# Transposing the next tile's attention output inside the last expert of the current tile

## What is computed

```python
# attention with a fixed decay mask per head (16 heads of 64), then a norm over
# each head's 64 channels and all 4096 positions, then the output projection
Q, K, V = (einsum('bld,hde->bhle', ln(x), W) for W in (Wq, Wk, Wv))
out = einsum('bhlm,bhme->bhle', (Q @ K^T) * Dm / sqrt(64), V)
c = head_norm(out) * gn_weight + gn_bias        # statistics over the whole sequence
x = x + c @ Wout
# mixture of experts: 8 routed (top 2, dense weights) and one shared, each 1024 -> 1408 -> 1024
h = ln(x)
combine = top2_softmax(h @ gate_w)
x = x + sum_e combine[e] * (silu(h @ w_gate[e]) * (h @ w_up[e])) @ w_down[e]
x = x + sigmoid(h @ shared_gate_w) * (silu(h @ sw_gate) * (h @ sw_up)) @ sw_down
```

## Time and profile before

| | us |
|---|---|
| median of the runs before | 6355.57 |
| lowest and highest of the two | 5952.12 and 6759.02 |
| the profiled execution | 5947.06 |
| its span, slowest core (core 7) | 5945.5 |
| spans of its eight cores | 5918.0 to 5945.5 |
| mean granted TensorE clock of the cores | 0.901 to 0.905 |

### The profile page before, as it was taken

One profiled execution on the slowest core, in us unless ns is written; L12 is line 12 of the kernel. 1 busy time (PEld: TensorE's weight loads), 2 busy tenths in 40 slices (PEclk: granted clock), 3 DMA queues, 4 the chain that ended last, 5 costly groups with the idle time before them and its releaser, 6 DMA issues.

```text
span 5945.5 us, 65497 instructions; the slowest of 8 cores (5918.0 to 5945.5 us)
## 1 busy us (share of the span) xinstructions
PE 5029.3 (85%) x24644; PEld 2342.1 (39%) x24644; DVE 1437.5 (24%) x3601; ACT 1439.3 (24%) x3555; POOL 190.0 (3%) x333
## 2 busy tenths in 40 slices
PE   3555555589998999899989998999899989998999
PEld 1333333334443444344434443444344434443444
DVE  1455544421112111211121112112211221122111
ACT  1343444221212121212121213121312131213121
POOL 0000000000000000000000000000000000000000
PEclk9666666689998999899989998999899989998999
DMA  8777777523342333343324343424242424242423
GB/s 173 179 180 178 180 184 181 152 93 158 134 153 117 158 134 152 118 160 132 154 116 166 126 156 116 173 117 166 113 166 117 167 114 164 117 169 91 163 117 131
DMA packets 101251, 867.26 MB, mean 146 GB/s; under 512 B 9552, under 2 KB 9552, under 8 KB 65360
## 3 DMA queue, kind: packets, MB, share of 16 engines
q0 software_dynamic: 76048, 787.00, 38.6%
q1 hardware_dynamic: 24896, 76.09, 3.7%
HBM read 837.91 MB, written 103.02 MB: 158 GB/s over the span
## 4 chain that ended last, share of the span: by engine, by line
PE 74%; ACT 3%; DVE 1%; issue 1%; DMA 0%; ACTq 0%; DVEq 0%; SPq 0%
PE psf L1025 25%; PE psf L968 23%; PE psf L972 23%; PE psf L831 2%; ACT silu_sb L984 1%; ACT xln_bf L161 1%; PE psb L750 1%; DVE h_sb L994 1%; ACT ucp_sb L985 1%; DMA x_sb<-x 0%; DVE combT L760 0%; DVE xln2T L764 0%; ACT L151 0%; ACT sqdump L132 0%; ACT sqdump L135 0%
## 5 line engine op out<-in xcount | busy, mean ns | idle before, releaser
L1025 PE MATMUL psf<-wring,h_sb 128*128 128x512 bf16 x6336 | 1464.7, 395 | 153.1 <-DVE h_sb L994 153.1
L968 PE MATMUL psf<-xln2T,wring 128*128 128x512 bf16 x6336 | 1510.2, 381 | 0.3 <-issue 0.2
L972 PE MATMUL psf<-xln2T,wring 128*128 128x512 bf16 x6336 | 1503.5, 380 | 0.0
L984 ACT ACTIVATE silu_sb<-psf 128x512 bf16<-128x512 f32 x792 | 472.9, 597 | 3288.9 <-PE psf L972 3288.9
L1025 PEld LDWEIGHTS psf<-wring,h_sb 128*128 128x128 bf16 x6336 | 636.0, 101 | 981.7 <-issue 301.7
L994 DVE TENSOR_TENSOR h_sb<-silu_sb,ucp_sb 128x512 bf16<-128x512 bf16 x792 | 336.9, 425 | 2429.4 <-ACT ucp_sb L985 2429.4
L972 PEld LDWEIGHTS psf<-xln2T,wring 128*128 128x128 bf16 x6336 | 622.2, 98 | 755.1 <-issue 13.4
L968 PEld LDWEIGHTS psf<-xln2T,wring 128*128 128x128 bf16 x6336 | 622.0, 98 | 754.0 <-issue 13.5
L1041 DVE SCALAR_TENSOR_TENSOR x_sb<-psf,c_sb,x_sb 128x512 f32<-128x512 f32 x576 | 432.6, 751 | 1120.1 <-PE psf L1025 1120.1
L985 ACT CAST ucp_sb<-psf 128x512 bf16<-128x512 f32 x792 | 459.6, 580 | 0.0
L254 PE MATMUL psb<-eye_sb,xln_bf 128*128 128x128 bf16 x256 | 32.3, 301 | 318.3 <-ACT xln_bf L161 311.9
(11 more groups left out here) (99 smaller groups left out, 1873.7 us busy)
## 6 DMA issues: line engine op xcount, KB each, us to landing
wring<-wbf POOLq DMA_DIRECT2D x216, 2816.0 KB, 10.4
wbf<-stg POOLq DMA_DIRECT2D x36, 1408.0 KB, 5.6
x_sb<-x SPq DMA_DIRECT2D x64, 512.0 KB, 6.0
stg<-wg POOLq DMA_DIRECT2D x16, 1408.0 KB, 11.3
stg<-wu POOLq DMA_DIRECT2D x16, 1408.0 KB, 11.2
out<-x_sb SPq DMA_DIRECT2D x32, 512.0 KB, 12.7
wbf<-stg POOLq DMA_DIRECT2D x9, 1536.0 KB, 6.0
stg<-wd POOLq DMA_DIRECT2D x8, 1536.0 KB, 12.4
```

Source lines behind the costliest of these rows:

```text
L968: t.matmul(gb, wring[:, wg0 + dt * IFF + it * C:wg0 + dt * IFF + (it + 1) * C], xln2T[:, dt * SC:(dt + 1) * SC], start=(dt == 0), stop=(dt ...
L972: ins = t.matmul(ub, wring[:, wu0 + dt * IFF + it * C:wu0 + dt * IFF + (it + 1) * C], xln2T[:, dt * SC:(dt + 1) * SC], start=(dt == 0), st ...
L984: sc.activation(silu_sb[:, (it % 2) * SC:(it % 2 + 1) * SC], gb, AF.Silu)
L1025: ins = t.matmul(db, h_sb[:, hb + it * SC + tloc * C:hb + it * SC + (tloc + 1) * C], wring[:, wd0 + it * D + dc * 512:wd0 + it * D + (dc + ...
```

## The change

The transposes of `combt_sb` for tile t_i + 1 are issued inside tile t_i, in the last expert (e = 8), between its last gate/up block and its first down group, by a new function `emit_combT_all`, with the same PSUM buffers, the same evictions and the same counters as before. The first of them waits for the load of the next rows of `comb` (`ldc_tgt`). At the start of a tile after the first, nothing is transposed, and the targets `combT_done` and `pet_tr_done`, which the output projection and `ldc` wait for, are those of the transposes in the tile before. On VectorE the eight evictions are queued behind the last expert's last product (L994) and ahead of its first accumulate (L1041). On the SP queue the order of the instructions is as before. The number of instructions that compute is the same.

```diff
--- before.py
+++ after.py
@@ -738,6 +738,34 @@
             emit_piece_load(p)
         next_piece = 3
 
+        def emit_combT_all(ld_tgt):
+            pe, vc = S("pet"), S("vct")
+            for dt in range(8):
+                reg = psb2[:, (dt % 2) * 1024:(dt % 2) * 1024 + 512]
+
+                def ttr(t, dt=dt, reg=reg, banktgt=vc.n - 1, ld_tgt=ld_tgt):
+                    if dt == 0:
+                        t.wait_ge(S("sld").h, ld_tgt)
+                    if banktgt >= 1:
+                        t.wait_ge(vc.h, banktgt)
+                    for tt in range(4):
+                        ins = t.transpose(reg[:, tt * C:(tt + 1) * C],
+                                          combt_sb[:, tt * D + dt * C:tt * D + (dt + 1) * C],
+                                          eye[:, :])
+                    ins.then_inc(pe.h, 1)
+                pe.n += 1
+                em("tensor", ttr)
+
+                def tev(v, dt=dt, reg=reg, tgt=pe.n):
+                    v.wait_ge(pe.h, tgt)
+                    ins = v.tensor_scalar(combT[:, dt * SC:(dt + 1) * SC], reg[:, :],
+                                          s12[:, dt:dt + 1], s12[:, 8 + dt:9 + dt],
+                                          ALU.mult, ALU.add)
+                    ins.then_inc(vc.h, 1)
+                vc.n += 1
+                em("vector", tev)
+            return pe.n, vc.n
+
         def emit_t512b(src_t, dst, scale_cols=None, shift_cols=None):
             pe, vc = S("pet"), S("vct")
             for dt in range(8):
@@ -769,6 +797,7 @@
         store_tgts = []
 
         wout_done_hist = {}
+        pipe2 = {}
         for t_i in range(NTILE):
             x1 = x1_sb[:, (t_i % 2) * 4 * D:(t_i % 2 + 1) * 4 * D]
             xcur = x_sb[:, (t_i % 2) * 4 * D:(t_i % 2 + 1) * 4 * D]
@@ -796,9 +825,13 @@
             em("vector", lambda v, tgt=combx_tgt: v.wait_ge(S("sld").h, tgt))
             em("scalar", lambda sc, tgt=combx_tgt: (sc.wait_ge(S("sld").h, tgt), sc.drain()))
 
-            emit_t512b(combt_sb, combT, s12[:, 0:8], s12[:, 8:16])
-            combT_done = S("vct").n
-            pet_tr_done = S("pet").n
+            if t_i == 0:
+                emit_t512b(combt_sb, combT, s12[:, 0:8], s12[:, 8:16])
+                combT_done = S("vct").n
+                pet_tr_done = S("pet").n
+            else:
+                combT_done = pipe2["combT_done"]
+                pet_tr_done = pipe2["pet_tr_done"]
 
             if t_i + 1 < NTILE:
                 S("sld").n += 64
@@ -811,6 +844,7 @@
                         ins.then_inc(S("sld").h, 16)
                     s.wait_ge(S("sld").h, tgt)
                 em("sync", ldc)
+                pipe2["ldc_tgt"] = S("sld").n
 
             vcw_tloc = []
             for tloc in range(4):
@@ -1003,6 +1037,10 @@
                 while next_piece < NPIECES and (next_piece - 3) in piece_done:
                     emit_piece_load(next_piece)
                     next_piece += 1
+                if e == NEXP - 1 and t_i + 1 < NTILE:
+                    petn, vctn = emit_combT_all(pipe2["ldc_tgt"])
+                    pipe2["combT_done"] = vctn
+                    pipe2["pet_tr_done"] = petn
 
                 for tloc in range(4):
                     for dc in range(2):
```

## The result

| | before | after |
|---|---|---|
| the profiled execution, us | 5947.06 | 5909.78 |
| its span, slowest core | 5945.5 | 5908.2 |
| mean granted clock of the cores | 0.901 to 0.905 | 0.906 to 0.907 |
| median of all executions, us | 6125.43 (10) | 6274.46 (11) |
| lowest execution, us | 5939.81 | 5899.46 |

The changed kernel takes 0.9939 of the time of before, with a 95% interval of 0.9918 to 0.996: 0.6% faster, some 36 us. The ratio leaves out the executions of either kernel in which the cores of one die or of both have a lower granted clock and take up to 14% longer; the two medians in the table include them and say nothing of the change.

What follows compares the result with a forecast made beforehand. Phase 2 was taken as a TensorE matmul stream, paying only for shorter holes or a higher clock. Seven boundaries of -3.7 us (-26) and -9 for the other experts' clock took 5947 to 5912 us; eight in ten between 5888 and 5943.

Steps and rivals of the forecast that it cites:

- removed stage: Start of a tile: transposes of 6.03 us go, a wait of 1.1 us shows; gain 4.9 us per boundary.
- clock of the output projection: Output projection after a pause of 1.1 us: its 64 matmuls keep the high clock, 13.9 instead of 16.21 us; gain 2.3.
- added stage: Last expert: 32 transposes ahead of the down matmuls make these start 3.5 us later per boundary.
- clock of the last expert: Last expert's down matmuls: one low-clock stretch as before, cost 0 per boundary, bounds -1.7 and +1.7 us.
- clock of the other experts: Holes ahead of the other eight experts' down matmuls: shorter tiles change how often the clock falls; -9 us in all.
- The rule cited: Last expert's transposes: the full clock does not engage for transposes, so they save no low stretch; otherwise 12 us less.
- What stands behind: VectorE, ScalarE, SP queue and POOL work behind the added transposes: no cost; without cover, a few us per tile.
- A: Rival: second low stretch in the last expert, output projection still starting low; +0.3 us per boundary, 5947 to 5949; chance 0.12.
- B: Rival: clock falls in the last expert and stays low through its down matmuls; +92 us, 6039; chance 0.02.
- C: Rival: last expert keeps its clock and all tiles become short ones; -54 us, 5893; chance 0.12.
- D: Rival: last expert's first transposes don't start in the hole; -27 us, 5920; chance counted within the forecast's 0.74.

Runs made afterwards that it cites:

- removed_only: The changed kernel without any transposes of comb after the first tile, every tile using the first tile's combT; ratio 0.9918 to the kernel before.
- cut16: The kernel before with 16 of the 64 output projection matmuls left out in every tile after the first; ratio 0.9973 to the kernel before.
- early_down: The kernel before, each expert's first down group starting on ten h blocks, waiting for the eleventh only ahead of its last matmul; ratio 0.965.

## Why the prediction was wrong, step by step

**What it forecast.** 5912 us was for "an execution like the profiled one", and there the time was 5909.78, with 36 us won where -35 stood. The median of all executions of the changed kernel is 6274.46 us, and that lies far outside 5888 to 5943. The step that failed there is the last one of the sum: the prediction saw 5952.12 and 6759.02 us, set the longer aside with "their median 6355.57 describes neither", and gave a range in which a time like it has no place. The runs showed that 7 of 11 executions took 6239.85 us or more, and 5 of 10 of the kernel before 6298.74 or more. No run shows that the change bears on that, and why an execution is of that length is open. As a statement on all executions the range was far too narrow; as one on the change it held, but two of its terms were mis-sized and one was missing, and these errors cancelled. The terms, summed over seven boundaries, against core 7:

| term | forecast, us | measured, us |
|---|---|---|
| removed stage | -34 | -33.3 |
| clock of the output projection | -16 | -13.1 (six of seven in the stretch) |
| added stage | +25 | +25.5 |
| clock of the last expert | 0 | -7.7 |
| clock of the other experts | -9 | -3.4 |
| first up matmuls behind the router | not in the sum | -4.3 |

**The removed stage**, -4.9 per tile: right. 6.03 - 1.27 = 4.76 us, and the exposed wait for L1079 was 1.11 to 1.27 us where 1.1 was said.

**The projection's clock**, -2.3: right. 16.21 to 13.97 us, in every tile looked at; removed_only shows that the pause of 1.27 us leaves the clock up.

**The added stage**, +3.5: right. 3.64 us, for the reason given: the third group waits for an eviction behind L1028. One reading in it was wrong without harm: two buffers hold two groups of four, so 8 transposes start in the hole and not 16, a quarter of them and not half. The sum went by the chain of evictions, which this doesn't touch.

**The clock of the last expert**, 0 with bounds of -1.7 and +1.7: wrong in size, -1.1 us per tile on core 7. One low stretch was expected as before, and there is one; but its cost was taken from the old place, where all of it lay on down matmuls. At the new place the clock was 0.53 from about 5281.7 to 5285.3, of which the down matmuls got 1.3 us. On other cores it went otherwise. On core 5 the clock stayed at 1.00 through the whole stage of transposes in three of seven last experts, and in the other four the down matmuls took 20.93 to 21.29 us, as much as before or more. Two of them (the stage of transposes, then the down matmuls):

```profile
1750.58:1756.26 5.68, 2.87 (x34) 1.90 (x32) 3.62 (x8) 1.07 (x2) 1.05 (x2) 1.00 0.47 155
1756.26:1775.41 19.15, 19.15 (x89) 8.48 (x88) 5.95 (x9) 0.00 (x0) 0.00 (x0) 1.00 0.65 257
...
2336.77:2342.69 5.92, 3.25 (x33) 2.36 (x32) 3.46 (x8) 1.07 (x2) 1.05 (x2) 0.79 0.50 171
2342.69:2363.98 21.29, 21.29 (x90) 9.04 (x88) 6.12 (x9) 0.00 (x0) 0.00 (x0) 0.90 0.57 224
```

The rule cited (TensorE: Matmul & The Clock Gate, Part 4: PE-mode transpose, of the Trainium skill) agrees with the trace of core 7 so far that the clock fell in spite of the transposes, and not with the first two rows here, where it stayed up through all 32 of them. It says nothing on where the low time then lies, and that was the money.

**The other experts' clock**, -9: wrong in size, and the total right only by accident. cut16 shows that a tile shortened by 3.45 us elsewhere leaves the count where it was. In the changed kernel the low stretches of the other experts fell from 37 to 35 of 56 on core 7, -3.4 us, and from 289 to 267 of 448 on all cores, -4.6 us per core; why they fell here and rose in removed_only is open. Had the term been left at 0 and the term above been sized at -1.1, the sum would have been nearly the same.

**What stands behind:** right. The SP queue's wait for the transposes is gone but for the first tile, no wait of the projection for combT appeared after the first tile, and on core 7 no wait for weights. Some other cores do wait for the weight DMA, in both kernels. The largest are cores 2 and 4 before, then core 4 after (us in total, times, longest):

```profile
PE psf L968 <- DMA wring<-wbf: 9.8, 13, 1.7
PE psf L968 <- DMA wring<-wbf: 5.3, 7, 1.1
...
PE psf L1002 <- DMA wring<-wbf: 12.8, 15, 2.4
```

Over the eight cores these waits are 15.1 us before and 19.2 after, so the change adds little, and "nothing" holds. But the weights were already close to late in the kernel before, which its core 7 does not show, and early_down ran into that limit.

**The rivals.** A is refuted by the 13.97 us. B and C did not come: no down stage ran wholly at the low clock, and the last expert of core 7 kept a short low stretch (in some last experts of cores 0, 3, 4 and 5 there was none, as C has it). D named a delay that didn't exist; the first group started at once.

## What to carry over

Work moved into a hole pays only for the part that needs nothing from the engine that makes the hole: here the evictions queued behind the very product that TensorE waited for, and 3.6 us came back of 4.8 us saved. Ask first whether the hole can be closed by reordering the consumer, since the first ten of eleven contraction steps needed nothing late: an edit of three lines won 3.5%, against 0.6% for the move. Then ask what the closed hole makes late, and price a low clock by what lies under it, not by its length. When a sum comes out, check its terms one by one: here the total was met to 1 us while three terms were off by 4 to 8 us.

## What had not been expected of the hardware

- Without holes the clock stays up through all down stages, on every core: on core 7 1207.0 us for 5544 matmuls of 128x512, 19.16 us per 88, with holes of 2.1 us 1280.7.
- A pause of 1.27 us between two dense stages never lowered the clock: in the changed kernel all seven projections behind such a pause took 13.97 us on core 7 and ran at the high clock on the other cores too. Pauses of 2.1 us lowered it in 44 of 63.
- Transposes at a thin occupation don't always take the clock down: in three of seven last experts of core 5 it stayed at 1.00 through the 5.7 us of the 32 transposes and their evictions.
- In the changed kernel the tiles of core 7 from the second to the seventh took 586.98 to 587.16 us each, where before they took 590.5 to 594.6: the low stretches had settled into one pattern. Why this one is open.
